# A four-layer tower kernel: keys stored ahead of queries, values projected late, the first triangular solve on all partitions

## What is computed

```python
# layer 0 (H = 4): l2-normed q, k; per token t
S = S + outer(k_t, (v_t - k_t @ S) * b_t);  o_t = q_t @ S
# layer 1 (H = 16): alpha_t decays every key channel
s = s * alpha_t[..., None]
s = s + b_t * outer(k_t, v_t - k_t @ s);    out_t = q_t @ s
y = x + rms(out) @ out_w * gate;  gate = sigmoid(silu(x @ u1_w + u1_b) @ u2_w + u2_b)
# experts: e = argmax(x @ wr + br);  y = gelu(x @ w1[e] + b1[e]) @ w2[e] + b2[e]
```

## Time and profile before

| | us |
|---|---|
| median of 3 runs (lowest, highest) | 832.8 (829.75, 835.26) |
| the profiled execution's own time | 832.5 |
| its span, first to last instruction | 830.4 |
| mean granted TensorE clock, share of full speed | 0.913 |

### The profile page before, as it was taken

The page is one execution under the profiler, slowest core; times in us unless marked ns, Lnnn a source line. Parts: engine busy times, 40 slices in busy tenths (PEclk is TensorE's granted clock), DMA queues, the critical chain, the costliest instruction groups (busy, mean ns, idle before and its releaser), DMA issues. The chain is left out here.

```text
span 830.4 us, 20092 instructions
## 1 busy us (share of the span) xinstructions
PE 696.5 (84%) x9130; PEld 519.2 (63%) x9130; DVE 360.0 (43%) x529; ACT 247.9 (30%) x467; POOL 158.0 (19%) x134
## 2 busy tenths in 40 slices
PE   8867157992999994879999999976679979999997
PEld 5546156782888883664466666655369966655554
DVE  0486954550111111251457666775944780421220
ACT  0461123120323220322034545424624443111033
POOL 9001001003000004400045555651013310000000
PEclk9978658995999996878999999999669999999999
DMA  9000000007998833000000002000000041000001
GB/s 343 23 1 1 0 2 2 1 2 279 355 336 297 331 127 114 1 1 19 1 21 23 23 22 73 4 3 2 0 2 5 4 185 72 1 1 0 1 1 39
DMA packets 19365, 56.39 MB, mean 68 GB/s; under 512 B 4177, under 2 KB 12241, under 8 KB 14929
## 3 DMA queue, kind: packets, MB, share of 16 engines
q1 hardware_dynamic: 18512, 53.01, 17.5%
q0 software_dynamic: 768, 2.10, 0.7%
HBM read 49.58 MB, written 5.52 MB: 66 GB/s over the span
## 5 line engine op out<-in xcount | busy, mean ns | idle before, releaser
L1325 PEld LDWEIGHTS PS<-arena 64*49 64x49 f32 x3584 | 63.0, 124 | 32.7 <-issue 20.4
L1325 PE MATMUL PS<-arena 64*49 64x48 f32 (+2 forms) x3584 | 71.4, 229 | 7.7 <-DVE arena L1555 5.3
L1284 PE MATMUL PS<-Y,arena 128*128 128x392 f32 x192 | 76.1, 527 | 0.4 <-DVE beta_tok L1508 0.4
L1533 DVE COPY_PREDICATED arena<-msk,PS 128x768 f32<-128x768 int32 x32 | 55.9, 1746 | 37.6 <-PE PS L1325 37.5
L216 PE MATMUL PS<-fill 128*128 128x256 bf16 x530 | 67.4, 281 | 3.3 <-DVE fill L1436 2.1
L216 PEld LDWEIGHTS PS<-fill 128*128 128x128 bf16 x530 | 51.9, 101 | 15.5 <-DVE fill L1436 2.1
L1234 PEld LDWEIGHTS PS<-arena 128*128 128x128 f32 x448 | 54.4, 199 | 2.4 <-issue 1.0
L1234 PE MATMUL PS<-arena 128*128 128x128 f32 x448 | 54.8, 283 | 1.2 <-DVE arena L1484 1.2
L972 POOL TENSOR_TENSOR arena<-arena 128x384 f32<-128x384 f32 (+1 forms) x32 | 38.6, 1206 | 87.7 <-PE PS L1325 87.6
L1032 ACT ACTIVATE arena<-PS,arena 128x128 f32<-128x128 f32 x112 | 31.9, 368 | 69.1 <-PE PS L1234 69.1
L366 POOL TENSOR_TENSOR arena<-arena,work 128x512 f32<-128x512 f32 x20 | 25.4, 1270 | 136.1 <-DVE work L650 136.0
(11 more groups left out here) (206 smaller groups left out, 1141.0 us busy)
## 6 DMA issues: line engine op xcount, KB each, us to landing
arena<-in_moe_w SPq DMA_DIRECT2D x28, 1024.0 KB, 6.4
arena<-in_qka_w SPq DMA_DIRECT2D x8, 384.0 KB, 3.1
arena<-in_patches SPq DMA_DIRECT2D x3, 784.0 KB, 6.4
arena<-in_ff_w SPq DMA_DIRECT2D x1, 2048.0 KB, 7.7
arena<-in_ffn_w SPq DMA_DIRECT2D x2, 1024.0 KB, 13.3
by_expert<-arena SPq DMA_DIRECT2D x1, 1792.0 KB, 13.4
arena<-in_moe_b SPq DMA_DIRECT2D x14, 128.0 KB, 6.8
arena<-by_expert SPq DMA_DIRECT2D x14, 128.0 KB, 2.5
```

The source lines that it names most:

```text
L1284: m = nc.tensor.matmul(bank(i % 3), GW[g % 2][:, k, u // 2], half(Y[:, k], u % 2), start=(k == 0), stop=(k == KT - 1))
L1325: m = nc.tensor.matmul(o, K[r, b, :], v, start=True, stop=True)
L1533: nc.vector.copy_predicated(dst, mk, src).then_inc(lv_kept, 1)
```

## The change

- First solve (`WideDelta`): the two blocks of both pictures of a pair lie on separate groups of 32 partitions, so all 128 are used and a step has n(i+1) elements. Rows come in by small products with slices of the identity, in two lots instead of twelve groups, and go out by products of 32 x 64.
- Experts: 14 slots for row tiles; SP loads tiles 3 to 13 right behind expert 1.
- Values: their weights are loaded after the last length sum into part of `work`; four tiles are projected in the last four steps of the levels, twelve in `pe_out` of the second solve; ACT keeps them.
- Levels: `KQ_SET` lies (kind, picture, token), keys first; one VectorE multiply makes first keys and queries; POOL's `first_keys` is gone; level k = 4 is kept by ACT in six copies; the multiplies for k = 3, 4, 5 are two instructions each. No fillers from tau 24.
- Sums, roots, lengths and beta columns of the second solve, and POOL's clears, run in steps 26 to 30 of the levels.
- The gate's u1 products and Silu run before the convolution ends, its u2 products and Sigmoids in the first five turns of the second `pe_apply`.

```diff
-        KQ_SET = [at(S0 + 4 * BT * i + BT, 2 * BT).rearrange("p (b t c) -> p b t c", b=B, c=2) for i in range(NSET)]
+        KQ_SET = [at(S0 + 4 * BT * i + BT, 2 * BT).rearrange("p (c b t) -> p c b t", c=2, b=B) for i in range(NSET)]
+        FIRST_SET = [at(S0 + 4 * BT * i, 3 * BT).rearrange("p (x n) -> p x n", x=3)[:, 0:3:2] for i in range(NSET)]
...
+        class WideDelta(Delta):
...
+            def block(self, cc, k):
+
+                s_ = 2 * cc + k
+                return slice(32 * s_, 32 * s_ + 32), slice(TP * cc, TP * cc + TP), \
+                    c("ident")[TP * cc:TP * cc + TP, TP * cc + BL * k:TP * cc + BL * k + BL]
...
+            def pe_rows(self, pe, n):
+
+                for t in (range(1, self.HALF), range(self.HALF, BL))[n]:
+                    for cc in range(2):
+                        for k in range(2):
+                            o, r, one_block = self.block(cc, k)
+                            a = (t - n * self.HALF) * BL
+                            m = nc.tensor.matmul(PS[o, n, a:a + BL], self.Am[r, :, min(BL * k + t, T - 1)], one_block,
+                                                 start=True, stop=True)
+                m.then_inc(self.s["turned_in"], 1)
...
+                for i in range(BL - 1):
+                    n = BL - 1 - i
+                    tmp = work[:, 0:n * (i + 1)].rearrange("p (t j) -> p t j", t=n)
+                    if i:
+                        self.wait(dve, "step", 2 * i)
+                    nc.vector.tensor_tensor(
+                        tmp, self.NSw[:, i + 1:BL, i:i + 1].broadcast_to([P, n, i + 1]),
+                        self.TSw[:, i:i + 1, BL:BL + i + 1].broadcast_to([P, n, i + 1]), ALU.mult) \
+                        .then_inc(self.s["step"], 1)
+                    self.wait(dve, "step", 2 * i + 1)
+                    rows_ = self.TSw[:, i + 1:BL, BL:BL + i + 1]
+                    nc.vector.tensor_tensor(rows_, rows_, tmp, ALU.subtract).then_inc(self.s["step"], 1)
...
+            def pe_out(self, pe):
+                S = self.S
+                for g in range(self.NGO):
+                    rows_ = min(4, BL - 4 * g)
+                    self.wait(pe, "step", 2 * (4 * g + rows_ - 1))
+                    if g >= 2:
+                        self.wait(pe, "u_kept", 2 * (g - 1))
+                    for r in range(rows_):
+                        for cc in range(2):
+                            for k in range(2):
+                                t = 4 * g + r
+                                if BL * k + t < T:
+                                    o, q_, _ = self.block(cc, k)
+                                    m = nc.tensor.matmul(PS[q_, 2 * (g % 2) + k, r * S:(r + 1) * S],
+                                                         self.TSw[o, t, BL * (1 - k):BL * (1 - k) + TP],
+                                                         c("ident")[o, o], start=True, stop=True)
+                    m.then_inc(self.s["turned_out"], 1)
...
         def later(x, h):
 
             if h == 32:
-                return x[:, 17:T].rearrange("p t c -> p c t").unsqueeze(2)
-            x = x[:, 1:T].rearrange("p (n two i) c -> p c n two i", two=2, i=h)[:, :, :, 1] if h <= 8 else                 x[:, 1:T].rearrange("p (n i) c -> p c n i", i=h)[:, :, 0:3:2]
-            return x
+                return x[:, :, 17:T].unsqueeze(2)
+            if h == 16:
+                return x[:, :, 1:T].rearrange("p c (n i) -> p c n i", i=h)[:, :, 0:3:2]
+            return x[:, :, 1:T].rearrange("p c (n two i) -> p c n two i", two=2, i=h)[:, :, :, 1]
...
+        TURNED = 7 * (FT // 2 - 1) + LAG + 2
+        V_TAIL = N_STEPS - TURNED - 1
+        V_AHEAD = (2, 2, 3, 3, 2 * BP - 10 - V_TAIL, 0, 0)
...
             load_expert(0)
             sp.wait_ge(scattered, 16 * BP)
             for j in range(3):
                 load_rows(j)
-            for j in range(1, NW):
+            load_expert(1)
+            for j in range(3, NT):
+                load_rows(j)
+            for j in range(2, NW):
                 load_expert(j)
             for j in range(NT):
                 sp.wait_ge(y_kept, j + 1)
                 sp.dma_start(answers[j * P:(j + 1) * P, :], YS[:, j % 2]).then_inc(stored[j % 2], 16)
-                if j + 3 < NT:
-                    sp.wait_ge(xt_mm, j + 1)
-                    load_rows(j + 3)
                 if j + NW < NT:
                     load_expert(j + NW)
-            sp.dma_start(VW, v_w).then_inc(loads["v1"], 16)
             for g in range(2, FT):
                 sp.wait_ge(g_mm, piece[g - 2, 5] + 1)
                 sp.dma_start(GW[g % 2], qka_w[g]).then_inc(g_loaded[g % 2], 16)
             sp.dma_start(OW, out_w).then_inc(loads["out_w"], 16)
...
+                if tau == TURNED:
+                    pool.wait_ge(lv_mm, unit[FT - NSET + 1, 6] + 1)
+                    delta1.pool_clear(pool)
...
+                    if k == 4:
+                        for n in range(3):
+                            m = nc.scalar.activation(dst[o:o + 9 + 16 * n, :, :, 9 + 16 * n:17 + 16 * n],
+                                                     src[o:o + 9 + 16 * n, :, :, 8 * n:8 * n + 8], ACT.Copy)
...
+            for n in range(2):
+                for k in range(KT):
+                    m = nc.tensor.matmul(bank(5 + n, slice(0, DH)), u1[:, k], half(X[:, k], n),
+                                         start=(k == 0), stop=(k == KT - 1))
+                m.then_inc(gate_mm, 1)
...
-                        spin(4, 0)
+                if tau == TURNED:
+                    pe.wait_ge(ss_kept, 1)
+                    delta1.pe_sums(pe, 3)
+                if tau == TURNED + 3:
+                    delta1.wait(pe, "rooted", 2)
+                    delta1.pe_cols(pe, 3)
+                if tau > TURNED:
+                    pe.wait_ge(loads["v1"], 16)
+                    value(tau - TURNED - 1)
...
+            def values_ahead(g):
+                o = V_TAIL + sum(V_AHEAD[:g])
+                for u in range(o, o + V_AHEAD[g]):
+                    value(u)
+
+            def gate_between(i):
+                u = i - 1
+                if 0 <= u < 4:
+                    pe.wait_ge(gate_act, 2 + u)
+                    nc.tensor.matmul(bank(7), u2[0:DH, (u // 2) * P:(u // 2 + 1) * P], sd[0:DH, u % 2],
+                                     start=True, stop=True).then_inc(gate_mm, 1)
+                if i == 5:
+                    pe.wait_ge(gate_act, 6)
+
+            delta1.pe_out(pe, values_ahead)
...
+            def first_moving(g):
 
                 dve.wait_ge(g_kept, piece[g, 5] + 1)
-                q_ = KQ_SET[g % NSET][..., 1]
-                nc.vector.tensor_tensor(q_, q_, DECAY_SET[g % NSET], ALU.mult).then_inc(lv_moving, 1)
+                nc.vector.tensor_tensor(KQ_SET[g % NSET].rearrange("p c b t -> p c (b t)"), FIRST_SET[g % NSET],
...
-                    v = moving[:, :, 33:T].rearrange("p b t c -> p b (t c)")
-                    end = ends[:, :, 32:33].broadcast_to([P, B, 32])
+                    v = moving[:, :, :, 33:T]
+                    nc.vector.tensor_tensor(v, v, over(ends[:, :, 32:33].broadcast_to([P, B, 16]), 2),
+                                            ALU.mult).then_inc(lv_moving, 1)
+                elif h == 2:
+                    v = moving[:, :, :, 2:T:2]
+                    nc.vector.tensor_tensor(v, v, over(ends[:, :, 1:T:2], 2), ALU.mult).then_inc(lv_moving, 1)
                 else:
-                    v = blocks_kq(moving, q)[:, :, :, 1]
-                    end = blocks(ends, q)[:, :, :, 0, q - 1:q].broadcast_to([P, B, 48 // h, 2 * q])
-                nc.vector.tensor_tensor(v, v, end, ALU.mult).then_inc(lv_moving, 1)
+                    end = blocks(ends, q)[:, :, :, 0, q - 1:q].broadcast_to([P, B, 48 // h, q])
+                    for cc in range(2):
+                        v = blocks(moving[:, cc], q)[:, :, :, 1]
+                        m = nc.vector.tensor_tensor(v, v, end, ALU.mult)
+                    m.then_inc(lv_moving, 1)
 
             for tau in range(N_STEPS):
...
+                if tau == TURNED - 1:
+                    dve.wait_ge(g_sum, FT)
+                    nc.vector.tensor_copy(ss[:, 0:HB, 0:T], bank(3)).then_inc(ss_kept, 1)
+                if tau == TURNED + 1:
+                    delta1.dve_lengths(dve)
+                if tau == TURNED + 4:
+                    delta1.dve_cols(dve, 3)
```

More of the change, by code:

```diff
@@ L709, in tower @@
         g_mm, g_copied, g_kept, g_sum, ss_kept = [sem("g_" + x) for x in ("mm", "copied", "kept", "summed", "sums_kept")]
[L710 to L711 removed]
+        lv_mm, lv_kept, lv_act, lv_moving, lv_keys, lv_ends = [
+            sem("level_" + x) for x in ("mm", "kept", "kept_act", "moving", "keys", "ends")]
         delta1 = Delta(delta0, H1, A1, PT1, W1, U1, D1, OT1, NS1, TS1, 0.0, 1e-6, 1e-6,
@@ L1188, in _ @@
             pe.wait_ge(pairs0_kept, 8)
-            delta0.pe_in(pe)
-            delta0.wait(pe, "rows_in", delta0.NGI)
```

(17 more changed lines are left out.)

302 lines of the change are left out of this document (172 added, 130 removed).

## The result

The changed kernel takes 784.5 us (median of 4 runs, 778.7 to 785.85), the kernel before 834.0 in the same session: ratio 0.940, 95% interval 0.934 to 0.946. It is 49.5 us faster; the forecast was 62.5, and 770. The profiled execution took 784.65 us with a span of 782.9, so 47.5 us of span are there to be explained.

What follows compares the result with a forecast made beforehand. Bounds differ by stage: VectorE in the solves, TensorE in experts, levels and apply. Terms -17.0, -4.0, -28.4, -8.4, -2.5, -5.0 and +2.8 sum to -62.5, taking 832.5 to 770 us; range 756 to 787.

Steps and rivals of the forecast that it cites:

- First solve: First solve spread over all partitions: shorter VectorE steps, cheaper entry, slightly dearer exit; -17 us (-12 to -19).
- rival B: First solve: TensorE holds the wide solve, its small products taking 25 us, not 14; 781 us, chance 0.10.
- Experts: Expert stage, rows loaded ahead: 5.6 us of row waits go, one new weight wait comes; -4 us (-1 to -5.6).
- rival E: Expert stage: expert 2 and 3 both late by a row load's queue; +2 instead of -4, 776 us, chance 0.05.
- Values late: Value projection moved into the last level steps and beside the second solve: -28.4 us (-27 to -29).
- Levels: Six level groups, keys ahead of queries: faster products less a new wait, -1.4 each; -8.4 us (+3 to -12).
- rival A: Levels: products get no faster while the longer VectorE step stalls each group; +3 for -8.4, 784 us, chance 0.16.
- The tail's -2.5: Rest of the levels after the six groups: a shorter chain of product, copy and multiply; -2.5 us (+1 to -4).
- Into the second solve: Preparation between the levels and the second solve: 14.3 us becomes 9.4; -5 us (-3 to -6).
- Gate: Gate: u1 products in TensorE's waits cost nothing, u2 products in the second apply's first heads cost +2.8 us (+2 to +4).
- Rival C: Solves and applies: the clock stays up, TensorE may enter both applies at 2.4 GHz; -5, 765 us, chance 0.09.
- D: Rival for the levels: TensorE falls to 1.2 GHz there and stays, making the kernel slower; 880 us, chance 0.02.

Runs made afterwards that it cites:

- experiment 5: The changed kernel with the first solve alone undone, four small systems side by side as before: 799.4 us, ratio 0.958.
- experiment 4: The changed kernel with the third expert's weights asked for before the later row tiles instead of behind them: 781.6 us, ratio 0.938.
- experiment 6: The changed kernel with keys and queries interleaved in memory again and the first multiply as two on VectorE: 800.4 us, ratio 0.961.
- experiment 9: The changed kernel with the first multiply split in two on VectorE, the keys' half ahead of the diagonal's copy: 775.9 us, ratio 0.926.
- experiment 1: The changed kernel with 48 filler products in TensorE's idle time at the end of the second solve: 774.1 us, ratio 0.9305.
- experiment 2: The changed kernel with the gate's four products and sigmoids moved from the apply into the second solve, no fillers: 771.0 us, ratio 0.926.
- experiment 8: The changed kernel with 98 filler products in TensorE's idle time in the first solve: 779.1 us, ratio 0.936.
- experiment 11: The kernel of experiment 10 with eight fillers behind each level product in the first three steps of the last two groups: 763.9 us, ratio 0.917.
- experiment 10: The changed kernel with the edits of experiment 2, experiment 4, experiment 8 and experiment 9 together: 763.9 us, ratio 0.915.
- experiment 7: The changed kernel with the keys' first multiply on GpSimd and the queries' on VectorE: 786.9 us, ratio 0.942.

## Why the prediction was right, and where it missed

The range and the direction hold; the forecast was 14.5 us too low.

- **First solve**: right, -16.65 for -17.0. 48 steps take 14.7 us for 14.0. The output groups take 1.08 us each, at half clock, where one is due every 2.2 to 2.8, so rival B is false. Undoing it alone brings the stage back to 40.1 us (experiment 5).
- **Experts**: right in kind, half the size. The row waits went (5.6 us); "a new wait of about 1.5 us, once" (its own 218.5 - 216.6 would have been 1.9) measured 2.86 for expert 2 and 0.86 for the one before, and 5.6 - 3.7 is near the 2.0 found (the stage alone scatters from 107.2 to 110.8 us, experiment 4, so a gain of 1.1 to 4.7). That is rival E's mechanism, at less than its price. Experiment 4 shows the row loads ahead of the weights as its cause.
- **Values late**: right, -28.4 for the place left, though the match to a tenth is luck: the same place takes 63.1 to 69.0 us in the other traces. The second solve stayed at 34.5 us.
- **Levels**: the products came out near the forecast (0.97, 0.97, 1.05, and 1.14 and 1.12 for k = 5 and 6: -1.7 a group for -1.9), and experiment 6 shows that the spacing alone does it; rival A is false. The pair level gained as much as the singles, so the sum "4 us smaller" that the prediction set beside its own did not come: the kernel puts tokens 3 and 4 of the first picture at floats 6 and 8 of the interleaved tile, on two sides of a 16-byte boundary counted from the tile's start. The term mis-sized is "a wait of 0.5 us per group": 0.98. Of the difference 0.3 is the multiply, put at 1.8 us and 2.12 long. The rest is TensorE coming sooner: the products of k = 0 and k = 4 ahead of the wait take 1.61 us up to the next projection and took 1.94. The forecast put nothing for k = 4, so this gain, 0.3 a group, was spent as wait. Experiment 9 shows that wait to be the one that counts. The tail's -2.5 was -0.35. Its trace has the lengths in VectorE's chain from 501.7 to 504.5, with TensorE waiting 0.81 us for the multiply behind them. That was read, not tried.
- **Into the second solve**: right, 9.55 us for 9.4.
- **Gate**: this is the largest term missed, and the step that failed: "8 records of 2.85/8 = 0.36 us, +2.8". It was +10.6. At full clock a record takes 0.46 us, and the four products with their waits 3.9 us (experiments 1 and 2): 1.1 more than forecast. The other 6.8 are the clock, 8.8 us lost in the changed kernel against 2.0 in the one before; with the stretch at 22.2 to 29.0 us in other traces that share is 3.7 to 10.5. The prediction had written down that the last eight microseconds of the second solve have no value left, but under rival C and as a reason why nothing is gained; it priced the gate by a row at full clock, in a place that it expected to start at half. The rows from the runs are 25.3 us as changed, 16.5 with the clock held, 12.6 with the gate out of the way.
- **Rival C** did not happen in the changed kernel, but its idea was right: with the clock up into the first apply (experiment 8) 2.8 us are gained, into the second 2.0 against the kernel before, 4.8 for its 5. D was far off: the six groups of the levels ran at clock 1.00.

Together: gate 7.8, levels 2.6, tail 2.1, experts 2.0, first solve and the rest 0.5: 15.0, the 62.5 - 47.5 of the two traces.

Open: what delays the clock's return between gate products, why the same edit held the clock in experiments 2 and 11 and not in 10, and the stages that no edit touches. From the last expert product to the first length sum the twelve experiments and the changed kernel take 63.1 to 69.0 us, with the changed kernel's own trace among the slowest. So the gain there may be larger than that trace's -28.4.

## What to carry to other kernels

When a change takes work off TensorE near a stage that it bounds, price that stage at the clock at which it will start, and look at what TensorE does in the last microseconds ahead of it: real work moved there (the gate) can be worth more than its own time, and fillers held the clock each time they stood there. Read such a stretch in several traces: the same code there took 22 to 29 us. Split a multiply that an engine must finish before the next product, and put the half that depends on nothing new ahead of the wait. Before giving work to GpSimd, look at which VectorE instructions of two inputs stand beside it.

## What the runs showed of the hardware

- The spacing of a float operand that TensorE streams costs time by itself: the 32 products (64 records) of 48 columns of k = 1 take 1.62 us where the columns are every fourth float (interleaved) and 0.97 where they are every second (experiment 6).
- VectorE and GpSimd hold each other up when both multiply: 0.57 us or less became 1.79 on GpSimd (changed kernel), 1.1 became 2.75 on VectorE (experiment 7).
- TensorE's granted clock fell in the 5.4 us after the last value product, with 1.1 us of work in them, and then stayed at 1.2 GHz through 19.1 us of the apply of which TensorE was busy 19.08. In other traces with the gate in that place it was back after 12 to 27 us. Without the gate between the heads the same low start lasted 4.8 us (kernel before) and 4.6 (experiment 10). That a clock once lost can stay away so long under full work I had not expected.
